# Graph edge sum on one core: the last batch of each sixteen written row by row, fewer but larger zero writes, the last chunk normalised on VectorE

## What is computed

```python
# x: 6250 x 128, feats: 206250 x 128, src: 206250 node numbers (not sorted)
edge_aggr = zeros((6250, 128)).at[src].add(feats)
h = concat([x, edge_aggr, glob]) @ W_c + b_c
h = softplus(h @ W1 + b1)
h = softplus(h @ W2 + b2)
out = layernorm(x + h @ W3 + b3)
```

## Time and profile before

| what | us |
|---|---|
| median of 3 runs | 1820.54 (1820.52 to 1820.98) |
| the profiled execution | 1821.66 |
| its span in the trace | 1819.8 |
| mean granted TensorE clock over the span | 0.984 |
| PE busy / DVE busy / POOL busy / ACT busy | 1753.7 / 1363.2 / 1204.4 / 1090.9 |
| L1093 matmuls (`move`), 9672 of them | 1171.0 |
| L495 indirect DMAs (`scatter`), 806 of them | 840.9 |
| L733 0/1 matrices on DVE, 1612 of them | 606.8 |

### The profile page before, as it was taken

The page is one execution under the profiler, slowest core; times in us unless marked ns, Lnnn a source line. Parts: engine busy times, 40 slices in busy tenths (PEclk is TensorE's granted clock), DMA queues, the critical chain, the costliest instruction groups (busy, mean ns, idle before and its releaser), DMA issues.

```text
span 1819.8 us, 63933 instructions
## 1 busy us (share of the span) xinstructions
PE 1753.7 (96%) x15337; PEld 1685.6 (93%) x15337; DVE 1363.2 (75%) x3893; ACT 1090.9 (60%) x3503; POOL 1204.4 (66%) x1542
## 2 busy tenths in 40 slices
PE   7899999999999999999999999999899999999985
PEld 4799999999999999999999999999899999999952
DVE  7877767777777777777777777777488888888855
ACT  1455555455555555555555555555488888888875
POOL 1577777777777777777777777777555555555548
PEclk9899999999999999999999999999899999999997
DMA  7388788877777777777777777777699999999912
GB/s 155 111 268 252 238 242 256 260 232 216 228 221 227 217 217 220 218 223 213 225 215 222 217 226 206 230 214 222 184 285 299 291 296 288 296 291 295 284 50 57
DMA packets 349559, 414.15 MB, mean 228 GB/s; under 512 B 28544, under 2 KB 249776, under 8 KB 347996
## 3 DMA queue, kind: packets, MB, share of 16 engines
q1 hardware_dynamic: 284003, 233.87, 46.0%
q0 software_dynamic: 57840, 176.38, 29.5%
q10 hardware_dynamic: 7689, 3.60, 1.1%
HBM read 233.69 MB, written 180.02 MB: 227 GB/s over the span
## 4 chain that ended last, share of the span: by engine, by line
PE 68%; POOL 10%; issue 8%; POOLq 6%; DMA 3%; ACT 1%; ACTq 0%; DVE 0%; SPq 0%; DVEq 0%
PE ps L1093 56%; PE ps L1170 7%; POOL sums L528 5%; POOLq L523 4%; DMA buckets<-arena,index 3%; POOL xn L557 2%; PE ps L1060 2%; PE ps L1066 2%; POOL buckets L495 2%; PE ps L1064 1%; POOLq L527 1%; POOLq L528 1%; POOLq L525 1%; DMA members<-buckets 0%; ACT arena L903 0%
## 5 line engine op out<-in xcount | busy, mean ns | idle before, releaser
L1093 PE MATMUL ps<-arena 128*120 (+1 forms) x9672 | 1171.0, 278 | 0.7 <-issue 0.5
L1093 PEld LDWEIGHTS ps<-arena 128*120 128x120 f32 x9672 | 1124.0, 183 | 1.2 <-issue 1.1
L495 POOL DMA_INDIRECT buckets<-arena,index x806 | 840.9, 1043 | 269.3 <-issue 225.5
L733 DVE TENSOR_SCALAR arena<-slot_no,slot_f 128x360 f32<-128x360 f16 x1612 | 606.8, 419 | 308.6 <-PE ps L1093 286.2
L903 ACT ACTIVATE arena<-ps 120x387 f32<-120x387 f32 x806 | 397.6, 493 | 563.3 <-PE ps L1093 484.4
L1170 PE MATMUL ps<-mark,members 128*128 128x128 f32 x3648 | 423.9, 278 | 9.2 <-ACT mark L990 7.0
L1170 PEld LDWEIGHTS ps<-mark,members 128*128 128x128 f32 x3648 | 417.0, 193 | 16.2 <-issue 8.9
L775 DVE TENSOR_SCALAR mark<-node_no,members 128x128 f32<-128x128 f16 x1368 | 357.1, 325 | 72.8 <-DMA members<-buckets 49.5
L528 POOL TENSOR_TENSOR sums<-sums,staged 128x128 f32 x456 | 219.8, 482 | 216.5 <-ACT staged L978 182.7
L869 ACT ACTIVATE reach<-block_no,arena 128x120 f16<-128x120 f16 x806 | 310.3, 386 | 0.6 <-PE ps L1103 0.6
L984 ACT ACTIVATE apart<-node_no,members 128x128 f32<-128x128 f16 x456 | 180.5, 396 | 19.4 <-DMA members<-buckets 11.8
(11 more groups left out here) (152 smaller groups left out, 591.5 us busy)
## 6 DMA issues: line engine op xcount, KB each, us to landing
members<-buckets SPq DMA_DIRECT2D x456, 258.0 KB, 3.5
arena<-in_feats SPq DMA_DIRECT2D x201, 512.0 KB
buckets<-arena,index POOLq DMA_INDIRECT x806
arena<-in_xT SPq DMA_DIRECT2D x12, 250.0 KB, 4.1
xn<-in_x ACTq DMA_DIRECT2D x1, 2800.0 KB
out_rows<-xn SPq DMA_DIRECT2D x12, 224.0 KB
arena<-in_src SPq DMA_DIRECT2D x1, 805.5 KB
buckets<-sums,end_now POOLq DMA_INDIRECT x50
```

The lines of the kernel that those rows point to most:

```text
L495: pool.indirect_dma_start(units, bass.IndirectOffsetOnAxis(ap=index[0:SLOTS, s, b:b + 1], axis=0), rows[0:SLOTS, o, :], None).then_inc(sca ...
L733: dve.tensor_scalar(perm[0:TP, b, t, :], slot_no[0:TP, :, :].rearrange("p r b -> p (r b)"), slot_f[0:TP, s % 2, b * TPB + t:b * TPB + t + ...
L1093: mm = pe.matmul(ps[0:SLOTS, MOVED + b, r * ROWF:(r + 1) * ROWF], perm[0:TP, b, t, r * SLOTS:(r + 1) * SLOTS], feat[0:TP, bass.ds(at, 1), ...
```

## The change

It has five parts.

1. **The last batch of each body is written directly.** Of batches 15, 31, ... 799 (`is_direct`), 50 in all, PE runs no `move`, DVE builds no matrices, and ACT fills no `rows` buffer. Instead `rank` of the body's last chunk adds two small f16 matmuls (`first_hi`, `first_lo`: the batch's first position in each bucket, split in two parts), so that the picked slot is already the row's place in its bucket list; DVE turns it into an index (`direct_at`), and POOL issues two indirect DMAs of 128 single rows of 516 bytes straight from `feat` (`scatter_direct`). They wait for the index and for the scatter of batch 7 of the body, the same stream. `firsts` on DVE makes the two tables once, before the loop.
2. **What waited for the last `move` waits for these DMAs.** The refill of the fourth slot of `feat` (`reload` on SP) and ACT's `set_locals` for it wait for `direct_landed`; counts of `moved`, `rows_ready` and `perm_made` run over 15 batches a body (`packed`). `take_rows` of batch 7 waits for the last body's direct rows.
3. **Local numbers are set later**: one chunk less ahead, at the fourth batch of a chunk and not at the first.
4. **Zero writes.** One indirect DMA clears the ends of four buckets, 16 rows for each partition, 32 partitions a bucket. There are 13 of these and the 12 spare ones as before, one a body for bodies 0 to 24 (`fill`), all of 1.06 MB. The copy of the column moves from POOL to ACT (`take_fill`, once a body, 25 times). The eighth gap write clears 18 rows and not 6. The small DVE work that finds the places (`zero_writes`) has 13 operations in place of 6.
5. **The last chunk is normalised on DVE**, with -mean made by a small DVE operation for each chunk (`less_mean`) and an addition in place of the subtraction.

PE's inner loop over half bodies of eight batches is gone; its loop body is now 16 batches, as it was on the other engines. ACT's body 0 stays outside the loops, and its loop over the bodies is split in two.

```diff
-    END_GAP = GAP - 1 + QR
+    PIECE = SPT * QR
+    PIECES = TROWS // PIECE
+    AT_ONCE = P // PIECES
+    ENDS = -(-KS // AT_ONCE)
+    FILLS = SPARES + ENDS
+    END_GAP = GAP - 1 + PIECE
...
+        def packed(i, k):
+            return i * (BODY - 1) + (k - k // BODY)
+        def is_direct(k):
+            return k % BODY == BODY - 1
...
+            def reload(i, s):
+                if s == XS - 1:
+                    sp.wait_ge(direct_landed, i * (16 * TPB))
+                else:
+                    sp.wait_ge(moved, packed(i, (s + 1 - XS) * CB))
+                load(i * XS + s, s, i * (XS // 2) + s // 2)
...
-            def end_of_bucket(i):
-                wait(pool, ends_zeroed, i * 16)
-                pool.tensor_copy(end_now[:, :], end_at[:, bass.ds(i, 1)]).then_inc(end_taken, 1)
-                pool.wait_ge(end_taken, i + 1)
+            def fill(i):
+                pool.wait_ge(fill_taken, i + 1)
                 if not isinstance(i, int):
                     pool.nop(nofuse=True)
                 pool.indirect_dma_start(
-                    units, bass.IndirectOffsetOnAxis(ap=end_now[:, :], axis=0),
-                    zero_src[:, 0:QR * ROWF], None).then_inc(ends_zeroed, 16)
+                    units, bass.IndirectOffsetOnAxis(ap=fill_now[:, :], axis=0),
+                    zero_src[:, 0:PIECE * ROWF], None).then_inc(filled, 16)
...
+            def scatter_direct(i):
+                pool.wait_ge(direct_ready, i + 1)
+                pool.wait_ge(scattered[STREAMS - 1], i * 16 + 32)
+                if not isinstance(i, int):
+                    pool.nop(nofuse=True)
+                for t in range(TPB):
+                    pool.indirect_dma_start(
+                        units, bass.IndirectOffsetOnAxis(ap=direct_at[0:TP, t:t + 1], axis=0),
+                        feat[0:TP, XS - 1, (CB - 1) * TPB + t, :], None).then_inc(direct_landed, 16)
...
             def scatter_body(i):
-                for s in range(XS):
-                    for b in range(CB):
-                        scatter(i * BODY + (s * CB + b), i * XS + s, s, b)
+                for k in range(BODY - 1):
+                    scatter(i, k)
+                scatter_direct(i)
...
+            def firsts():
+                dve.wait_ge(places_made, 1)
+                at_ = count_f[0:K, 0:BODIES * BODY].rearrange("p (i k) -> p i k", k=BODY)[:, :, BODY - 1]
+                dve.tensor_scalar(first_i[0:K, :], at_, 1.0 / P, None, ALU.mult).then_inc(firsts_a, 1)
...
+                if is_direct(k):
+                    turn = i + k // BODY
+                    wait(dve, direct_landed, turn * (16 * TPB))
+                    dve.tensor_scalar(direct_at[0:TP, :], slot_f[0:TP, s, b * TPB:(b + 1) * TPB], float(RUNITS), None,
+                                      ALU.mult).then_inc(direct_ready, 1)
+                    return
...
+                if s == XS - 1:
+                    body = i
+                    pe.wait_ge(firsts_made, 2)
+                    for part, table in ((first_hi, ident128_16[0:K, :]), (first_lo, ident2_16[0:K, 0, :])):
+                        pe.matmul(out_[:, CB - 1, :, :], part[0:K, bass.ds(body, 1)].to_broadcast([K, TP]),
+                                  table.unsqueeze(1).to_broadcast([K, TPB, K]), start=False, stop=False)
...
+            def take_fill(i):
+                wait(act, filled, i * 16)
...
+                act.activation(fill_now[:, :], fill_at[:, bass.ds(i, 1)], ACT.Copy).then_inc(fill_taken, 1)
...
+            t0, nt = chunks[NCH - 1]
+            dve.wait_ge(shift_ready, NCH)
+            for t in range(nt):
+                part = xn[:, (t0 + t) * D:(t0 + t + 1) * D]
+                dve.tensor_scalar(part, part, newt[0:NP_, (NCH - 1) % 2, 2, t:t + 1], newt[0:NP_, (NCH - 1) % 2, 1, t:t + 1],
+                                  ALU.mult, ALU.add).then_inc(last_normed, 1)
```

More of the change, by code:

```diff
@@ L740, in _ @@
+            permutation(0, 1)
+            firsts()
             dve.wait_ge(base_a, 1)
@@ L870, in reached, with indices @@
                    .then_inc(reach_made, 1)
-            def indices(c, s, turn):
+            def indices(c, s, turn, body):
                 n = CB if not isinstance(c, int) else chunk_batches(c)
@@ L875, in indices @@
                 if not isinstance(c, int) or c >= XS:
-                    for b in range(CB):
+                    for b in range(CB - s % 2):
                         act.wait_ge(scattered[s % 2 * CB + b], turn * 16)
+                    if s == 1:
+                        act.wait_ge(scattered[STREAMS - 1], 16 + body * 16)
                 act.activation(index[0:SLOTS, s, 0:n], ps[0:SLOTS, GOTO + s % 2, 0:n], ACT.Identity,
@@ L887, in _, with set_locals @@
                .then_inc(ends_copied, 1)
-            def set_locals(c, s):
-                wait(act, moved, (c + 1 - XS) * CB)
-                n = (CB if not isinstance(c, int) else chunk_batches(c)) * TPB
-                if not isinstance(c, int):
+            def set_locals(i, s):
+                c = i * XS + s
+                if s % XS == XS - 1:
+                    wait(act, direct_landed, (i + s // XS) * (16 * TPB))
+                else:
+                    wait(act, moved, packed(i, (s + 1 - XS) * CB))
+                n = (CB if not isinstance(i, int) else chunk_batches(c)) * TPB
+                if not isinstance(i, int):
@@ L905, in _ @@
+            def take_fill(i):
+                wait(act, filled, i * 16)
+                if not isinstance(i, int):
+                    act.nop(nofuse=True)
+                act.activation(fill_now[:, :], fill_at[:, bass.ds(i, 1)], ACT.Copy).then_inc(fill_taken, 1)
             act.wait_ge(local_a, 2)
-            for c in range(XS - 1):
-                set_locals(c, c)
+            for c in range(XS - 2):
+                set_locals(0, c)
             for g in range(RS, AHEAD):
                 reached(g, g % RS)
-            indices(0, 0, 0)
@@ L912, in take @@
-            def take(g, b, c, s, turn):
-                ends = isinstance(g, int)
-                if b == 0 and (not ends or c + XS - 1 < CHUNKS):
-                    set_locals(c + (XS - 1), (s + XS - 1) % XS)
-                if b == 1 and (not ends or c + 1 < CHUNKS):
-                    indices(c + 1, (s + 1) % XS, turn + (s % 2 + 1) // 2)
-                take_rows(g, b, s, turn)
-                if not ends or g + AHEAD < NBAT:
-                    reached(g + AHEAD, (s * CB + b + AHEAD) % RS)
@@ L922, in take_body, with take @@
-            def take_body(i):
-                for s in range(XS):
-                    for b in range(CB):
-                        take(i * BODY + (s * CB + b), b, i * XS + s, s, i * (XS // 2) + s // 2)
-            take_body(0)
-            with act.Fori(1, BODIES - 1) as i:
-                take_body(i)
+            indices(0, 0, 0, 0)
+            def take(i, k):
+                ends = isinstance(i, int)
+                s, b = k // CB, k % CB
+                c = i * XS + s
+                if b == CB - 1 and (not ends or c + XS - 2 < CHUNKS):
+                    set_locals(i, s + (XS - 2))
+                if b == 1 and (not ends or c + 1 < CHUNKS):
+                    indices(c + 1, (s + 1) % XS, i * (XS // 2) + (s + 1) // 2, i + (s + 1) // XS)
+                if not is_direct(k):
+                    take_rows(i, k)
+                if not ends or k + AHEAD < NBAT:
+                    reached(i * BODY + (k + AHEAD), (k + AHEAD) % RS)
@@ L930, in _ @@
+            for k in range(BODY):
+                take(0, k)
+            act.wait_ge(fill_at_made, 1 + AT_ONCE)
+            take_fill(0)
+            with act.Fori(1, FILLS) as i:
+                for k in range(BODY):
+                    take(i, k)
+                    if k == 2 * CB:
+                        take_fill(i)
+            with act.Fori(FILLS, BODIES - 1) as i:
+                for k in range(BODY):
+                    take(i, k)
             for g in range((BODIES - 1) * BODY, NBAT):
-                take(g, g % CB, g // CB, g // CB % XS, g // STREAMS)
+                take(0, g)
@@ L1072, in _ @@
             rank(0, 0)
-            rank(1, 1)
+            rank(0, 1)
             pe.wait_ge(places_made, 1)
@@ L1130, in _ @@
             with pe.Fori(1, BODIES - 1) as i:
[L1131 to L1135 removed]
+                for k in range(BODY):
+                    work(i, k)
             for g in range((BODIES - 1) * BODY, NBAT):
[L1137 to L1138 removed]
+                work(0, g)
             pe.wait_ge(index_ready, CHUNKS)
```

264 lines of the change are left out of this document (141 added, 123 removed).

## The result

The changed kernel takes 1764.1 us at the median (1762.8 to 1767.4), the kernel before 1820.8 beside it: a ratio of 0.969, 95% interval 0.968 to 0.971. I forecast 1776 us in 1745 to 1808. Direction and mechanism are those of the forecast; the gain is 56 us and not 44.5. The profiled execution took 1763.5 us with a span of 1761.6, against a span of 1819.8 before.

The account below looks back on a forecast made before the run. The prediction took POOL's indirect DMAs to bound the loop's fill bodies and PE the rest. Terms of -0.6 (body 0), -42.3 (loop), -1.9 (tail) and +0.3 (prologue) gave -44.5 us, so 1776 us, range 1745 to 1808.

Parts of the forecast that it names:

- What bounds it: Batch loop: POOL's indirect DMAs set bodies with a fill (24.34 us), PE the others (23.11 us), with POOL close at 22.98.
- PE's body: PE's time per batch-loop body: 24.35 us less one move of 1.335 plus 0.10 for added matmuls, giving 23.11 us.
- the two f16 matmuls: Matmuls of 98 columns added to rank on PE: taken at 0.10 us, between 0.07 by columns and 0.18.
- POOL's DMA: Batch loop: each indirect DMA costs POOL 1.352 us whatever its size, bounds 1.29 and 1.39 us.
- Edits at nothing: Batch loop: take_fill, fewer DVE matrices, late set_locals, zero_writes (under 2 us once) and SP's refill were costed at nothing.
- The loop's sum: Batch loop, bodies 1 to 49: 584.2 plus 577.8, together 1162.0 us against 1204.26, 42.3 us less.
- What POOL may be behind at the end of the loop: End of batch loop: POOL's lag might shrink by about 3 us or not; left at nought.
- The tail: Last chunk's normalisation moved from POOL to DVE: four scalings in 1.2 us, saving 1.9 us (bounds 1.5 and 2.4).
- Rival 1: Batch loop: POOL held up at every DMA, 1.39 us each, loop only 12.4 us less, 1806 us; chance 0.14.
- Rival 2: Batch loop: PE waits 4.3 us for features refilled after direct DMAs; 1957 us if in all 49 bodies; chance 0.05.
- Rival 3: Batch loop: PE's doubled loop body stalls at the jump for instruction fetch, about 3.3 us a body, 1908 us; chance 0.05.
- Rival 4: Batch loop: POOL does not bind, DMAs at 1.29 us, PE's 23.11 us holds throughout, 1746 us; chance 0.12.

Follow-up runs that it names:

- fills_no_direct: The changed kernel without the direct rows, all 16 batches of a body packed and scattered; merged zero writes and tail edit stay: 1794.3 us, ratio 0.986.
- The two padded kernels: Memsets on POOL ahead of its sum loop: eight in the changed kernel, 1774.5 us (ratio 0.974); 60 in the kernel before, 1810.5 us (0.994).
- before_add: The kernel before with POOL's normalisation as multiply and add on a negated mean, in place of multiply and subtract: 1815.8 us, ratio 0.997.
- after_last_on_pool: The changed kernel with its last chunk normalised on POOL again, with multiply and add: 1764.8 us, ratio 0.970.
- before_pad60: The kernel before with 60 one-column memsets on POOL ahead of its loop of sum additions: 1810.5 us, ratio 0.994.
- short_perm: The changed kernel with DVE writing only 8 of 360 columns of each 0/1 matrix in bodies 1 to 48 (wrong results): 1751.2 us, one execution.
- long_turns: The changed kernel with POOL's sum loop turning 14 times over 32 steps, not 56 over 8: 2059.1 us on the slow chip, 1761.7 us on another.

## Why the prediction was right, and where not

**What bounds it: right, and too narrow.** POOL with its 1.352 us a DMA, and PE close behind it, are what the loop obeys. The step that failed was to stop there: I cut only the batch loop by stages and took the other stages as fixed. The chain of before had 10% in POOL and 6% in its queue, and I read these as the loop's, where they were mostly the sum stage's.

**PE's body: 23.11 forecast, 23.24 measured.** The term that was mis-sized is the two f16 matmuls at 0.10 us, with 0.18 named as the other end. Taking a move's 1.335 us off the 24.35 leaves 23.01, so they and their loads cost some 0.23 us. In the timeline of the weight loads it is 0.31: from the first load of `rank` to the next `move` a chunk takes 0.67 us with them (1235.24 to 1235.91) and 0.36 without. Both are outside my bounds; PE's loads pause for 0.24 us ahead of the new tables, which columns do not count. It cost 24 x 0.13 = 3.1 us. In fills_no_direct the body without them is 24.35 us still, so nothing else of the change slows PE.

**POOL's DMA: 1.352 forecast; 24.26 / 18 = 1.348 measured.** A saving of 1.9 us against the forecast, with the clean stretches of before as the right source. The new DMAs cost the same at 516, 1548 and 8256 bytes.

**Edits at nothing: one was not.** `zero_writes` lies at a place where POOL had rows waiting, as I wrote, but PE had nothing to spare there. DVE's `hotc` came behind it. From the timeline of PE, at the end of body 0:

```profile
90.75 0.34 PE L1162 MATMUL ps<-hotc,tri 128*128 128x392 f16 x1 [1.76 <-DVE hotc L633]
```

That and POOL's own wait behind it make the first interval 25.82 us, 1.5 over the 24.34 of the forecast. `take_fill`, the late `set_locals` and SP's refills did cost nothing: PE is busy for all of the 557.83 us of the later bodies.

**The loop's sum: right.** -40.4 against -42.9 us, of which +3.1 is PE's body, +1.5 the first interval, -1.9 POOL's price. What POOL may be behind at the end of the loop, which I left at nought, did not show.

**The sum stage: -9.7 against 0, the largest miss.** It was not weighed, neither as a term nor as a rival. The two padded kernels show its cause, the place of POOL's loop. The 16% of POOL and its queue in the chain of before were for the most part this stage, which is why they are gone in after.

**The tail: -8.2 against -1.9.** The term held four scalings of one chunk and missed the other 46: I counted what moved to DVE and not that `subtract` became `add` for all of them, with POOL back to back in this stage. before_add gives 4.1 us to that, after_last_on_pool 1.0 us to DVE (four operations of 1.11 us in all, against 1.2 forecast). The other 3.1 us lie at the head of the tail: POOL ended its additions 1.1 us less behind PE, and PE's clock did not fall to 0.50. Why POOL is less behind at that point is open; the place of its loop alone does not do it, since before_pad60 keeps a tail of 80.6 us. The tail of fills_no_direct, 76.1 us with the clock at 1.00 in its head, does not speak against this: its head takes 8.5 us, and it ends 6.4 us after the last scaling, where after ends 2.9 us after it.

**The rivals.** Rival 1, POOL held up at every DMA: not at 1.39 us. Less work on DVE took 42 ns off each scatter in short_perm, so something of DVE's does hold POOL up a little. The Trainium skill, SBUF — State Buffer, section "SBUF: two separate sides", says that GpSimd cannot write its descriptors while VectorE is in a two-port mode; that fits the direction, but no run isolates that mode. Rival 2: PE never waited for its features in the later bodies, though SP's refill waited for direct rows 49 times. Rival 3: 28 instruction packets against 27, and no gap at PE's jump; dead. Its idea did live on another engine, at a price of 0.02 us a step on average. Rival 4: POOL does bind, with PE idle for 10 us of the fill bodies. The range held the time by the sum of two opposite kinds of error: the loop's small ones against me, and two stages that I had not opened in my favour.

## What to carry to other kernels

Cut every stage into its steps before you forecast, also those that the diff does not touch, and look in each for the engine whose steps repeat at a fixed pace: where that engine's program shifts, its loops may become quicker or slower, and here that was a sixth of the gain. An indirect DMA cost the issuing engine the same 1.35 us here for rows of 516 to 8256 bytes, so count them before you hand it work, and pair a change that adds some with one that takes some away. Where an operand's sign is free, time both forms.

## What the runs showed of the hardware that I had not expected

- POOL's loop of 8 additions takes 7.44 us a turn where the kernel before has it, and 7.26 eight instructions earlier or 60 later, for the same instructions. Only 28 packets of instructions were fetched in the whole run of after and 27 in before, so nothing is fetched again over a queue that the profile shows. The Trainium skill, Runtime: NRT & Kernel Launch, section "Instruction fetch mechanics", ties the price of a taken branch to whether its target is buffered; here a jump cost 0.25 us more than a plain step in the quick places and 0.44 us over two steps in the slow one.
- POOL's scaling of 125x128 f32 takes 792 ns with `mult, subtract` and 448 ns with `mult, add` (454 in the kernel before with that edit alone). DVE takes 343 ns.
- A DMA of POOL takes 1.03 us for 128 rows of 516 bytes and 1.02 us for 8256 bytes a row.
- One chip ran the kernel before in 2063.9 us, where the others took 1819 to 1821, and two changed kernels gained 0.3 and 0.9% there and not 3 to 4%. The trace of one of them, long_turns, has the stretches in which PE took a load every 0.70 us, and PE was busy for 1067 of 1200 us in its batch loop. What holds PE up is not in the profile; the changed kernel itself was not run there.
- PE's matmuls of 500 columns at the head of the tail take 1.88 us for two in before at a granted clock of 0.50, and 1.00 us in after at 1.00. PE had idled for 2.45 us just ahead in the one and for 1.33 us in the other.
